# A graph layer on one core: 70 batches by count matrices instead of 67, and two gathered groups instead of three in some of them

## The reference, cut to what matters

```python
def _L1_gnn_ref(x, edge_index, W, b, gamma, beta):
    xw = x @ W
    ...
    dinv = jnp.where(deg > 0, jax.lax.rsqrt(deg), 0.0)
    norm = dinv[src] * dinv[dst]
    msg = xw[src] * norm[:, None]
    out = jax.ops.segment_sum(msg, dst, num_segments=N) + b
    mean = jnp.mean(out, axis=0)
    var = jnp.mean((out - mean) ** 2, axis=0)
    out = (out - mean) * jax.lax.rsqrt(var + BN_EPS) * gamma + beta
    return jax.nn.relu(out)
```

## Time and profile before

| | us |
|---|---|
| median of 3 runs | 7344.63 |
| lowest and highest | 7341.11 and 7347.38 |
| the profiled execution's own time | 7344.54 |
| span of its profile | 7342.8 |

### The profile page before, as it was taken

One profiled execution on the slowest core, in us unless ns is written; L12 is line 12 of the kernel. 1 busy time (PEld: TensorE's weight loads), 2 busy tenths in 40 slices (PEclk: granted clock), 3 DMA queues, 4 the chain that ended last, 5 costly groups with the idle time before them and its releaser, 6 DMA issues. The chain is left out here.

```text
span 7342.8 us, 156129 instructions
## 1 busy us (share of the span) xinstructions
PE 5812.5 (79%) x41800; PEld 4127.1 (56%) x41800; DVE 5317.5 (72%) x14198; ACT 3558.1 (48%) x5657; POOL 5086.9 (69%) x5375
## 2 busy tenths in 40 slices
PE   7778787877788777777777765676999999999994
PEld 6555555555556555555555544554666666666662
DVE  7777777777778888888888873456777777777765
ACT  2555555555555555555555550063333333333334
POOL 4577777777777777777777774435777777777770
PEclk6565666666656888887777776677999999999995
DMA  4222222221223444443333327724222222222222
GB/s 129 80 85 85 86 86 72 57 57 56 57 57 99 119 118 119 122 115 98 96 98 99 97 75 234 240 95 141 77 75 77 77 76 76 76 77 76 76 77 73
DMA packets 512129, 695.39 MB, mean 95 GB/s; under 512 B 255298, under 2 KB 367644, under 8 KB 510878
## 3 DMA queue, kind: packets, MB, share of 16 engines
q1 hardware_dynamic: 317008, 347.69, 16.9%
q0 software_dynamic: 181376, 321.40, 14.9%
q10 hardware_dynamic: 13498, 24.07, 1.0%
HBM read 450.80 MB, written 241.85 MB: 94 GB/s over the span
## 5 line engine op out<-in xcount | busy, mean ns | idle before, releaser
L1694 POOL DMA_INDIRECT msg_tab<-big x3224 | 3159.3, 980 | 1065.3 <-issue 1041.2
L2245 POOL DMA_INDIRECT big<-y_parts,big x1616 | 1590.1, 984 | 551.5 <-issue 487.1
L2326 ACT CAST big<-ps 128x980 bf16<-128x980 f32 x804 | 783.9, 975 | 1277.8 <-PE ps L2274 1276.8
L2286 PE MATMUL ps<-big 128*128 128x384 bf16 x6566 | 1199.4, 326 | 0.2 <-ACT big L2326 0.2
L2378 DVE TENSOR_SCALAR big<-big,dstF 128x343 bf16<-128x343 f16 (+2 forms) x3216 | 985.3, 338 | 235.7 <-PE ps L2274 129.5
L1383 ACT CAST big<-ps 128x512 bf16<-128x512 f32 x403 | 236.0, 586 | 1511.2 <-DMA msg_tab<-big 1507.4
L2286 PEld LDWEIGHTS ps<-big 128*128 128x128 bf16 x6566 | 581.7, 97 | 350.0 <-issue 3.9
L1178 PE MATMUL ps<-big 2*128 2x512 bf16 x806 | 336.3, 509 | 547.6 <-ACT big L1367 547.4
L1186 PE MATMUL ps<-big 128*128 128x128 f32 x3224 | 706.5, 390 | 10.9 <-ACT big L1378 7.2
L1186 PEld LDWEIGHTS ps<-big 128*128 128x128 f32 x3224 | 635.4, 293 | 20.2 <-ACT big L1378 20.0
L1491 DVE TENSOR_REDUCE big<-big 128x8 f32<-128x784 f32 x403 | 629.9, 1563 | 0.0
(11 more groups left out here) (289 smaller groups left out, 10746.0 us busy)
## 6 DMA issues: line engine op xcount, KB each, us to landing
arena<-msg_tab SPq DMA_DIRECT2D x97, 727.5 KB, 4.4
big<-msg_tab SPq DMA_DIRECT2D x97, 630.5 KB
big<-in_edge_attr SPq DMA_DIRECT2D x403, 128.0 KB
msg_tab<-big POOLq DMA_INDIRECT x3224
big<-msg_tab SPq DMA_DIRECT2D x97, 388.0 KB
msg_tab<-big SPq DMA_DIRECT2D x97, 291.0 KB
big<-y_parts,big POOLq DMA_INDIRECT x1616
big<-h_parts SPq DMA_DIRECT2D x403, 48.0 KB
```

Source lines behind the costliest of these rows:

```text
L1694: nc.gpsimd.indirect_dma_start(out=m.msg_tab[:, :], out_offset=bass.IndirectOffsetOnAxis(ap=sidx[s][:, j:j + 1], axis=0), in_=row[s][:, j, ...
L2245: nc.gpsimd.indirect_dma_start(out=m.grow[s][:, 3 * D * j:3 * D * j + 3 * D], out_offset=None, in_=m.y_parts[:, :], in_offset=bass.Indirec ...
L2286: mm = pe.matmul(ps_rows, m.cnt[h][:, a, :], m.y_part[:, HALF * h + a, :], start=(h == 0 and a == 0), stop=(h == 1 and a == HALF - 1))
L2326: nc.scalar.copy(m.cnt[h][:, :, SLOTS * i:SLOTS * i + SLOTS].rearrange("p h (a w) -> p h a w", a=2), ps_cnt[i % 2][:, :, 0:SIDE * HALF].re ...
```

## The change

67 batches become 70 (210 groups by counts), and 202 gathered groups become 193. The loop over batches now has a body of 11 batches and runs six times; batch 0 stands ahead of it and three batches behind it. In each turn of the loop batches 3, 7 and 11 take two gathered groups, after steps 5 and 11, and the other eight take three, after steps 3, 7 and 11 as before. One gathered group stays ahead of all batches. The place table of a batch number grows by three columns, and the views behind it move by three or four; some views of the setup are packed more closely to make room for the longer list of bounds. What a count, a window, a pick or a gather is does not change.

```diff
-BIG = 33084
+BIG = 33088
...
-NBT = 67
+NBT = 70
 DENSE = NBT * GB
-KP = 3
+TURN = (3, 3, 2, 3, 3, 3, 2, 3, 3, 3, 2)
+TURNS = 6
+PLACED = {3: (3, 7, 11), 2: (5, 11)}
 NPG = G - DENSE
-KEEN = NPG - KP * NBT
+KEEN = NPG - TURNS * sum(TURN) - 3 * (NBT - TURNS * len(TURN))
...
-            with eng.Fori(0, (NBT - 3) // 2) as i:
-                for c in (1, 2):
+            with eng.Fori(0, TURNS) as i:
+                for c in range(1, len(TURN) + 1):
                     for h in range(2):
-                        unit(2 * i + c, i, c, h, False, False)
-                    done(2 * i + c)
-            for c in (NBT - 2, NBT - 1):
+                        unit(len(TURN) * i + c, i, c, h, False, False)
+                    done(len(TURN) * i + c)
+            for b in range(TURNS * len(TURN) + 1, NBT):
                 for h in range(2):
-                    unit(c, 0, c, h, False, c == NBT - 1)
-                done(c)
-
-        def gathered_in(b, i, c, h, step):
-            k = (6 * h + step) // 4
-            n = KEEN + KP * c + k
-            return KEEN + KP * b + k, n % 2, 3 * i + n // 2, n % 3
+                    unit(b, TURNS, b - TURNS * len(TURN), h, False, b == NBT - 1)
+                done(b)
+
+        def windows_of(c, pair):
+            return TURN[c - 1] if 0 < c and not isinstance(pair, int) else 3
+
+        def gathered_in(pair, c, k):
+            n = KEEN + k + (3 if c else 0)
+            for d in range(1, c):
+                n += windows_of(d, pair)
+            return sum(TURN) * pair + n, n % 2, sum(TURN) // 2 * pair + n // 2, n % 3
...
-                    if (6 * h + i) % 4 == 3:
-                        n, s, turn, _ = gathered_in(b, pair, c, h, i)
+                    placed_at = PLACED[windows_of(c, pair)]
+                    if 6 * h + i in placed_at:
+                        n, s, turn, _ = gathered_in(pair, c, placed_at.index(6 * h + i))
                         window(n, s, turn)
...
-                    if step % 4 == 0:
+                    count = windows_of(c, pair)
+                    k, at = step // (12 // count), step % (12 // count)
+                    n, s, _, t = gathered_in(pair, c, k)
+                    if at == 0:
                         picks(n, s)
-                        if not (last and step == 8):
+                        if not (last and k == count - 1):
                             indices(n + 1, (t + 1) % 3)
-                    if step % 4 == 1:
-                        add_window(n - 1, 1 - s, b + 1 if h or i == 5 or first else b)
+                    if at == 1:
+                        add_window(n - 1, 1 - s, b + 1 if step > 2 or first else b)
```

More of the change, by code:

```diff
@@ L240, in __init__ @@
         self.place = self.big[:, 32768:32768 + NBT]
-        self.gidx = [self.big[:, 32835 + J * t:32835 + J * t + J].bitcast(U32) for t in range(3)]
+        self.gidx = [self.big[:, 32838 + J * t:32838 + J * t + J].bitcast(U32) for t in range(3)]
         self.turn = [self.big[:, 18816 + 2048 * t:20864 + 2048 * t] for t in range(4)]
-        self.iota_half = self.big[:, 32860:33084].bitcast(F16)
+        self.iota_half = self.big[:, 32864:33088].bitcast(F16)
         self.sel = self.big[0:CB, 27008:27008 + P]
@@ L330, in setup_stages @@
     mid = m.spare[:, 84:84 + 8]
[L331 to L335, removed]
+    tile_min = m.spare[:, 92:124]
+    tile_max = m.spare[:, 124:156]
+    tile_off = [m.spare[:, 156:188], m.spare[:, 188:220]]
+    bounds = m.spare[0:1, 220:220 + 2 * DENSE]
+    limits = m.spare[0:1, 81:84]
     flag_f = work[0:1, 5900:5901]
@@ L2390, in unit @@
                     step = 6 * h + i
-                    n, s, _, t = gathered_in(b, pair, c, h, i)
                     if not (last and h):
                         hots(CB * (u + 1) + i, b + h, 1 - h, i)
-                    if step % 4 == 0:
+                    count = windows_of(c, pair)
+                    k, at = step // (12 // count), step % (12 // count)
+                    n, s, _, t = gathered_in(pair, c, k)
+                    if at == 0:
                         picks(n, s)
-                        if not (last and step == 8):
+                        if not (last and k == count - 1):
                             indices(n + 1, (t + 1) % 3)
-                    if step % 4 == 1:
-                        add_window(n - 1, 1 - s, b + 1 if h or i == 5 or first else b)
+                    if at == 1:
+                        add_window(n - 1, 1 - s, b + 1 if step > 2 or first else b)
                     if step == 2 and not first:
```

## The result

| | before | after |
|---|---|---|
| median of 4 runs each, us | 7344.77 | 7289.65 |
| lowest and highest after, us | | 7280.21 and 7294.00 |
| the profiled execution's own time, us | 7344.54 | 7280.21 |
| its span, us | 7342.8 | 7276.9 |

What follows compares the result with a forecast made beforehand. The prediction took POOL's gather issues as the bound: 7344.5 us, less 93.6 for nine gathered groups fewer, plus 14 for PE's stops at the loop's branches, gives 7265 us, with a range of 7246 to 7300.

Steps and rivals of the forecast that it cites:

- POOL is the bound, nine groups are worth 93.6 us: Batches of graph_layer: POOL's gather issues set the end, so nine gathered groups fewer at 10.40 us save 93.6 us.
- Three more batches fit into PE's waits: PE in the batch loop: former waiting, 2.7 us a batch, covers three more batches, leaving 2.8 us a turn.
- Rival B: PE in the batches becomes the bound: at 3% slower steps 38 us come back, 7303 us; chance 0.22.
- The branch stops PE: At five branches back of the longer loop PE stands still 3.4 us plus 1.6 slow clock; 14 us lost.
- Rival A: Batch loop: POOL alone sets the pace and the branch costs nothing, 7251 us; chance 0.20.
- How far PE may fall behind: Within a turn PE may be 8.7 us behind before POOL stops; 7.2 is the most, so nothing is lost.
- Density of DVE beside POOL: Batches: DVE's denser work may lengthen POOL's issues, 0 to 5 us, left to the range.
- C: PE's straight-line loop body is fetched too late, 391 us more, 7642 us in all; chance 0.05.
- D: The check for fewer than 128 destinations a batch fails, the stage runs another way, much longer; chance 0.01.

Runs made afterwards that it cites:

- the repeats: The changed kernel run again without any edit, once in each of two sets: 7285.45 us and 7287.99 us.
- e5_spread: Changed kernel with its loop kept, two-group batches moved away from the branch, to places 3, 6 and 9 of the turn: 7272.08 us.
- e2_pe_straight: Changed kernel with PE's loop over batches written out straight, other engines keeping the loop: 7268.61 us.
- e4_before_ten: Kernel before, with a loop body of ten batches instead of two: 7344.69 us, ratio 0.9992.
- e7_few_picks: Kernel before, with DVE making one of the eight picks of a group behind batch 0, that part of the computation left out: 7338.69 us.
- e1_again: The changed kernel run again without any edit, in the first set: 7285.45 us.
- the straight kernel: The kernel of e2_pe_straight: changed kernel with PE's loop over batches written out, no branch on PE: 7268.61 us.

## Why the prediction was right, and where it was off

**POOL is the bound, nine groups are worth 93.6 us: right.** Nine groups, 72 issues, at the pace of before, are 93.7 us in the traces.

**Three more batches fit into PE's waits: right, to the hundredth.** From window to window PE takes 9.30 to 9.31 and 9.86 us when nothing holds it. Its waits for rows went from 130.7 us to 20.8. Rival B, PE slower than in batch 0, did not come.

**The branch stops PE: right in kind, place and size.** Five stops of 2.53 to 3.03 us, 315 to 319 us apart, where 3.4 and 312 were forecast; q8 moves in the middle of the stage; behind the stop shown above one slow step of 3.62 us, 1.7 more than usual, where 1.6 was taken from the earlier trace rows, but none behind two of the five. In all a branch costs PE 3.9 us in this profile and 4.5 in each repeat; the prediction had 3.4 to 5.0, and its 14 us of loss stand for 4.3. That a body of two batches brings neither the stop nor packets on q8 and one of ten brings both is shown by the kernel before with ten batches. Rival A is refuted by the same rows.

**How far PE may fall behind: wrong, the step that failed.** The prediction had 8.7 us, from "the rows of a group are there 1.63 us after its last issue". The rows of before show that this took the wrong issue for the last:

```profile
5717.57 1.00 POOL L2245 DMA_INDIRECT big<-y_parts,big  x1 [0.30 <-issue]
```

This one is the group's last; the one at 5718.87 is the first of the next group. Rows are used 5720.50 - 5717.57 = 2.9 us after the last issue starts. The second slip is that POOL doesn't start when the window ends but 0.8 us later: in the profile after 15 groups start 0.80 to 0.83 us behind the end of a window, and none sooner. The next-but-one group would start 1.30 + 10.40 = 11.7 us after the last issue; less 2.9 for the rows, 1.5 for the window and 0.8 for POOL's start leaves 6.5 us. The branch shown above has both: the last issue at 5741.58, rows usable at 5744.5, the window at 5754.91, so 10.4 behind, and POOL's step was 5.21 us instead of 1.26, so 3.95 lost, and 10.4 - 3.95 = 6.5. The same working at the 20 waits over 0.5 us in the three profiles of the changed kernel gives 6.1 to 6.9.

With 6.5 the balance of the turn reads otherwise. A batch with two groups alone puts PE 6.33 us behind, and the changed order has one right ahead of every branch. The tightest place is the first window behind the branch, and not the third batch. That could have been seen without a run: by the prediction's own numbers PE would be 6.33 + 5.0 = 11.3 us behind right there, over its 8.7 already. Of a branch's cost 3.1 us are lost in this profile and 3.7 in the repeats, where 14 / 5 = 2.8 was forecast. Two more waits stand elsewhere, of 2.12 and 2.14 us. The one at 6582 is in the seventh batch, behind a stretch of low granted clock (0.52 to 0.62) that followed a wait of PE for rows of 2.57 us; the other, at 6784, is in the third batch behind the last branch, the place that the prediction named. In sum 19.2 us are lost in this profile and 22.3 and 20.5 in the repeats, where 14 were forecast. Moving the two-group batch off the branch (e5_spread) and removing the branch (e2_pe_straight) each bring POOL's waits beyond ordinary steps to 2.0 us or less.

**Density of DVE beside POOL: mis-sized.** Priced at 0 to 5 us and left out of the sum, it measured 5.7 us between the first two profiles and 11 to 12 between e4_before_ten and the repeats (0.0071 to 0.0079 us on 1,527 steps). That less work on DVE makes POOL's issues faster is what e7_few_picks speaks for, and by its slope DVE's busy time is only part of the amount; what the rest is stays open.

**The sum, mended.** With the trace of e4_before_ten as before: -93.4 (72 x 1.2977) + 12.1 for the other steps + 22.3 for the waits = -59.0, where the stage of e1_again is 59.5 us shorter and its median 62.4 under before. The prediction had -79.6; of the 17 to 20 us between, some 8 are POOL's waits beyond the 14 that were forecast (22.3 and 20.5, so 8.3 and 6.5), by the limit that was taken too wide, and 11 to 12 are the slower issues.

**Rivals.** C, slower by late code: refuted by the straight kernel. B did not come, although the time fell near its end of the range. D did not come: the stage has 1,544 gathers, 193 groups.

## What to carry to other kernels

Two engines that hand buffers to each other are balanced over a turn only if at each place of it the one is no further behind than the buffers reach; so measure that reach from both ends, from the start of the last issue to the use of its data and from the end of the use to the restart, and walk the order with it. An engine whose work was hidden by waiting has stops that cost nothing until the waiting is gone: before filling it, look for what else lay in it, here the branch of a longer loop body. Where two uneven things have to be placed, a branch and a short batch, keep them apart; moving two short batches a place or two was worth 16 us, as much as removing the branches.

## What the hardware showed that I had not expected

- A branch back over a body of ten or eleven batches stops PE for 2.3 to 3.2 us with "issue"; the same instructions in a straight line, with 39 packets on q8 in 600 us, cost nothing (window to window 9.86 us).
- DVE's stops at the turn of its loop, 3.4 us each, 31 times before, show in no row of the longer bodies: its one-hots there have 1.3 us of "issue" in six pieces. That they fall into DVE's waits for PE is likely but not shown. e7_few_picks bears on it: there the loop of two batches turns as before and q14 still moves 49 packets in 600 us, but DVE, with less to do, waits for PE 295.9 us at its one-hots (128.4 before) and has no such stop.
- POOL resumes 0.80 us after the end of the window that it waited for, in every profile in which it waited, and no group started sooner.
- POOL's issue depends on what the other engines do: 971 ns with an eighth of the picks, 975 to 978 before, 981 after. It differs between chips as well: 986 to 989 in the third set, of which no kernel before has a trace.
